# Attention plus gated FFN on one core: the last batch's third gate and up moved ahead of the products of the batch before it, batch 0's third gate and up given a bank pair that is free earlier, and the last scores put behind V products and zeros

## The reference, cut to what matters

```python
qkv = x @ w_qkv                                   # x (8, 512, 128), w_qkv (128, 384)
att = softmax(where(causal, q @ k.T / sqrt(8), -inf))
x = layernorm(x + att @ v)
gate = x @ (w_gate / 127).T; up = x @ (w_up / 127).T      # (8, 512, 384)
x = layernorm(x + (silu(gate) * up) @ (w_down / 127).T)
```

## Time and profile before

| | us |
|---|---|
| median of 3 executions | 364.29 |
| lowest, highest of them | 361.03, 364.29 |
| the profiled execution, its own time | 362.71 |
| span of its profile (first to last instruction) | 361.0 |
| attention, up to the last score matmul | 0 to 296.4 |
| from there to the first matmul of `gate_up(1, 0)` | 296.4 to 306.9 |
| FFN of the batches 1 to 7 up to the last matmul | 306.9 to 353.1 |
| last norm and store | 353.1 to 361.0 |

### The profile page before, as it was taken

One profiled execution on the slowest core, in us unless ns is written; L12 is line 12 of the kernel. 1 busy time (PEld: TensorE's weight loads), 2 busy tenths in 40 slices (PEclk: granted clock), 3 DMA queues, 4 the chain that ended last, 5 costly groups with the idle time before them and its releaser, 6 DMA issues.

```text
span 361.0 us, 9029 instructions
## 1 busy us (share of the span) xinstructions
PE 338.2 (94%) x2907; PEld 198.4 (55%) x2911; DVE 291.8 (81%) x1247; ACT 214.6 (59%) x277; POOL 180.2 (50%) x329
## 2 busy tenths in 40 slices
PE   4878999999999999999999999999999998999971
PEld 2533445556455645655564556556445544898961
DVE  6875658898888888988988898899898884868653
ACT  2400447877777677777867676876677774434310
POOL 8400133653384455447335734653433578787552
PEclk9996559999999999999999999999999969999997
DMA  4798330276337426532661553166200010011111
GB/s 145 279 301 246 83 86 5 63 254 190 91 126 229 120 63 236 155 112 86 228 190 37 188 170 120 33 237 202 66 4 5 5 30 3 1 36 53 46 44 58
DMA packets 33902, 41.73 MB, mean 116 GB/s; under 512 B 3136, under 2 KB 17472, under 8 KB 33856
## 3 DMA queue, kind: packets, MB, share of 16 engines
q1 hardware_dynamic: 33856, 41.17, 36.0%
HBM read 21.76 MB, written 18.87 MB: 113 GB/s over the span
## 4 chain that ended last, share of the span: by engine, by line
PE 79%; DVE 9%; issue 5%; DMA 3%; ACT 2%; POOL 1%; SPq 0%; DVEq 0%; POOLq 0%; ACTq 0%
PE psum L500 21%; PE psum L477 18%; PE psum L460 14%; PE psum L681 5%; DVE masked L853 5%; PE psum L416 5%; PE psum L407 4%; PE psum L669 3%; PE psum L671 3%; PE psum L442 2%; PE psum L509 2%; PE psum L432 2%; DMA scr_k<-parts 1%; DVE nm L853 1%; DMA xa<-L_attn_x 1%
## 5 line engine op out<-in xcount | busy, mean ns | idle before, releaser
L853 DVE CUSTOM_DVE_ANT_0 masked<-psum,mask 128x384 bf16<-128x384 f32 (+3 forms) x512 | 219.2, 487 | 37.5 <-PE psum L477 30.6
L756 ACT ACTIVATE pt<-psum 128x1024 f32<-128x1024 f32 x160 | 158.4, 1021 | 59.7 <-PE psum L460 59.2
L1028 POOL TENSOR_SCALAR_AFFINE_SELECT pt<-pt 128x512 f32<-128x512 f32 x128 | 79.7, 635 | 101.5 <-ACT pt L756 99.5
L477 PE MATMUL psum<-kx,qx 33*128 33x384 f32 (+3 forms) x512 | 93.5, 366 | 3.3 <-DMA kx<-scr_k 1.8
L500 PE MATMUL psum<-pt,vx 128*32 128x256 f32 (+2 forms) x1280 | 94.8, 397 | 0.1
L460 PE MATMUL psum<-qx,kx 35*128 35x384 f32 (+3 forms) x512 | 77.7, 353 | 0.9 <-DMA qx<-nm_T 0.8
L477 PEld LDWEIGHTS psum<-kx,qx 33*128 33x128 f32 x512 | 54.3, 193 | 40.9 <-DVE nm L853 19.1
L460 PEld LDWEIGHTS psum<-qx,kx 35*128 35x128 f32 x512 | 47.2, 192 | 30.4 <-issue 16.1
L500 PEld LDWEIGHTS psum<-pt,vx 128*32 128x32 f32 x1280 | 30.7, 110 | 39.0 <-issue 26.0
L853 DVE DVE_READ_ACCUMULATOR2_ANT nm<- 128x1 f32 x512 | 42.5, 83 | 0.0
L1016 POOL TENSOR_SCALAR nm_parts<-nm 128x16 fp32r<-128x16 f32 x32 | 6.6, 207 | 51.4 <-DVE nm L853 50.3
(11 more groups left out here) (64 smaller groups left out, 268.6 us busy)
## 6 DMA issues: line engine op xcount, KB each, us to landing
scr_q<-parts SPq DMA_DIRECT2D x16, 512.0 KB, 3.7
scr_k<-parts SPq DMA_DIRECT2D x16, 512.0 KB, 5.5
qx<-scr_q SPq DMA_DIRECT2D x64, 128.0 KB, 2.6
kx<-scr_k SPq DMA_DIRECT2D x64, 128.0 KB, 2.7
xa<-L_attn_x SPq DMA_DIRECT2D x8, 256.0 KB, 3.3
res<-L_attn_x SPq DMA_DIRECT2D x8, 256.0 KB, 2.8
out<-yo SPq DMA_DIRECT2D x8, 256.0 KB, 2.3
qx<-nm_T SPq DMA_DIRECT2D x64, 8.0 KB
```

Source lines behind the costliest of these rows:

```text
L477: last = pe.matmul(bank[:, col:col + width], qx[u][at:at + KM, 2 * g + hh // 2, P * i:P * i + P].bitcast(F32R), kx[u][at:at + KM, 2 * g + ...
L756: act.activation(pt[G % 2][:, 2 * s:2 * s + 2, :], pair_of("S", G, s), ACT.Exp, scale=SM_SCALE).then_inc(exp_done, 1)
L853: dve.tensor_tensor_reduce(masked[count % 4][:, 0:width], bank[:, col:col + width], mask[:, T - width:T], -1.0, 3.0e38, ALU.add, ALU.min, ...
L1028: pool.affine_select(out=blocks, in_=blocks, pattern=[[0, HG], [1, P]], compare_op=ALU.is_ge, fill=0.0, base=0, channel_multiplier=-1).the ...
```

## The change

**TensorE.** V products "0a" of group 30 go ahead of scores(31, 0), and three matmuls of zeros between them; "0b" ahead of scores(31, 1); two zeros ahead of scores(31, 2); "1" ahead of scores(31, 3). In the FFN, the bank pair of gate_up becomes a function of batch and m: batch 0 has pairs 0, 1, 0 for m = 0, 1, 2, the later batches 1, 2, 0, so that gate_up(0, 2) waits only for hidden(0, 0), and stands ahead of turn_out(15) instead of behind it; the wait for `attn_made` 16 and `ot_copied` 16 goes to gate_up(1, 1). For batch 7, gate_up(7, 2) goes ahead of down(6), and down(7) writes bank 6 instead of bank 4, with waits for the x1 of batch 7 instead of `r2_made`.

**VectorE.** hidden(7, 2) goes ahead of residual2(6); the norm of batch 6 is applied here (last_norm2(6)), behind residual2(7) and ahead of last_norm2(7).

**GpSimd.** For batch 6 only inverse2(6) is left.

```diff
--- before.py
+++ after.py
@@ -299,9 +299,17 @@
 
 
 
-        x1_ps, y_ps = psum[:, 6, :], psum[:, 4, :]
+        x1_ps = psum[:, 6, :]
+
+        def y_ps(c):
+            return psum[:, 4, :] if c < B - 1 else x1_ps
+
         last_pair = SCORE_TURNS.index(("S", GROUPS - 1, SLOTS - 2)) % 2
-        ff_ps = [(psum[:, 2 * p, :], psum[:, 2 * p + 1, :]) for p in (last_pair, 1 - last_pair)] + [(psum[:, 5, :], pv_ps)]
+        ff_pairs = [(psum[:, 2 * p, :], psum[:, 2 * p + 1, :]) for p in (last_pair, 1 - last_pair)] + [(psum[:, 5, :], pv_ps)]
+
+        def ff_ps(c, m):
+
+            return ff_pairs[(0, 1, 0)[m] if c == 0 else (1, 2, 0)[m]]
 
         block = ctx.enter_context(nc.Block())
 
@@ -656,42 +664,51 @@
                     transposes4(x1_ps, res[:, NB * c:NB * c + NB, :].rearrange("p n c -> p (n c)")).then_inc(x1_turned, 1)
 
             def gate_up(c, m):
-                if c > 0:
+                if c > 1:
                     pe.wait_ge(hid_made, HC * (c - 1) + m + 1)
-                elif m < 2:
-                    pe.wait_ge(exp_done, SLOTS * GROUPS - 1 + m)
-                else:
+                elif c == 1 and m == 1:
                     pe.wait_ge(attn_made, 2 * B)
                     pe.wait_ge(ot_copied, 2 * B)
+                elif c == 1:
+                    pe.wait_ge(hid_made, 2 + m // 2)
+                elif m == 2:
+                    pe.wait_ge(hid_made, 1)
+                else:
+                    pe.wait_ge(exp_done, SLOTS * GROUPS - 1 + m)
                 for n, full in enumerate((gate_full, up_full)):
                     w = wT[:, n, P * m:P * m + P].bitcast(F32R)
                     pe.wait_ge(x1_hi_made, c + 1)
-                    pe.matmul(ff_ps[m][n], w, x1_hi[c % 2][:].bitcast(F32R), start=True, stop=False)
+                    pe.matmul(ff_ps(c, m)[n], w, x1_hi[c % 2][:].bitcast(F32R), start=True, stop=False)
                     pe.wait_ge(x1_lo_made, c + 1)
-                    pe.matmul(ff_ps[m][n], w, x1_lo[c % 2][:].bitcast(F32R), start=False, stop=True).then_inc(full, 1)
+                    pe.matmul(ff_ps(c, m)[n], w, x1_lo[c % 2][:].bitcast(F32R), start=False, stop=True).then_inc(full, 1)
 
             def down(c):
                 pe.wait_ge(hid_made, HC * c + HC)
                 if c == 0:
                     pe.wait_ge(attn_made, 2 * B - 1)
+                elif c < B - 1:
+                    pe.wait_ge(r2_made, c)
                 else:
-                    pe.wait_ge(r2_made, c)
+                    pe.wait_ge(x1_hi_made, B)
+                    pe.wait_ge(x1_lo_made, B)
                 for m in range(HC):
                     for n in range(NB):
-                        last = pe.matmul(y_ps[:, C * n:C * n + C], hid[c % 2][:, m, P * n:P * n + P],
+                        last = pe.matmul(y_ps(c)[:, C * n:C * n + C], hid[c % 2][:, m, P * n:P * n + P],
                                          wT[:, 2, P * m:P * m + P], start=(m == 0 and n == 0),
                                          stop=(m == HC - 1 and n == NB - 1), skip_group_check=True)
                 last.then_inc(y_full, 1)
 
 
             G = GROUPS - 1
+            values(G - 1, "0a")
+            add_zeros(3)
             scores(G, 0)
-            values(G - 1, "0a")
+            values(G - 1, "0b")
             scores(G, 1)
-            values(G - 1, "0b")
+            add_zeros(2)
             scores(G, 2)
+            values(G - 1, "1")
             scores(G, 3)
-            values(G - 1, "1")
             turn_x1(0)
             scores(G, 4)
             turn_out(2 * B - 2)
@@ -702,14 +719,17 @@
             gate_up(0, 1)
             values(G, "2")
             turn_x1(1)
+            gate_up(0, 2)
             turn_out(2 * B - 1)
-            gate_up(0, 2)
             for c in range(1, B):
                 gate_up(c, 0)
                 gate_up(c, 1)
+                if c == B - 1:
+                    gate_up(c, 2)
                 turn_x1(c + 1)
                 down(c - 1)
-                gate_up(c, 2)
+                if c < B - 1:
+                    gate_up(c, 2)
             down(B - 1)
 
         @block.scalar
@@ -814,7 +834,7 @@
                 act.wait_ge(gate_full, k + 1)
                 if k > 1:
                     act.wait_ge(hid_made, k - 1)
-                act.activation(sg[k % 2][:], ff_ps[m][0], ACT.Silu, scale=W_SCALE).then_inc(silu_done, 1)
+                act.activation(sg[k % 2][:], ff_ps(c, m)[0], ACT.Silu, scale=W_SCALE).then_inc(silu_done, 1)
 
             for s in range(SLOTS - 1):
                 exp_slot(GROUPS - 1, s)
@@ -940,14 +960,14 @@
                         dve.wait_ge(pv_piece, PIECES * (GROUPS - 1 + c))
                     else:
                         dve.wait_ge(y_full, c - 1)
-                dve.tensor_tensor(hid[c % 2][:, m, :], ff_ps[m][1], sg[k % 2][:], ALU.mult).then_inc(hid_made, 1)
+                dve.tensor_tensor(hid[c % 2][:, m, :], ff_ps(c, m)[1], sg[k % 2][:], ALU.mult).then_inc(hid_made, 1)
 
             def residual2(c):
                 u = c % 2
                 dve.wait_ge(y_full, c + 1)
                 if c > 1:
                     dve.wait_ge(yo_made, NB * (c - 1))
-                dve.scalar_tensor_tensor(r2[u][:].rearrange("p n c -> p (n c)"), y_ps, W_SCALE * W_SCALE,
+                dve.scalar_tensor_tensor(r2[u][:].rearrange("p n c -> p (n c)"), y_ps(c), W_SCALE * W_SCALE,
                                          res[:, NB * c:NB * c + NB, :].rearrange("p n c -> p (n c)"),
                                          ALU.mult, ALU.add).then_inc(r2_made, 1)
                 dve.wait_ge(r2_made, c + 1)
@@ -980,10 +1000,14 @@
                 hidden(c, 1)
                 if c == 1:
                     stats1(B - 1)
+                if c == B - 1:
+                    hidden(c, 2)
                 low_x1(c + 1)
                 residual2(c - 1)
-                hidden(c, 2)
+                if c < B - 1:
+                    hidden(c, 2)
             residual2(B - 1)
+            last_norm2(B - 2)
             last_norm2(B - 1)
 
         @block.gpsimd
@@ -1121,10 +1145,11 @@
             norm1(3, 2)
             inverse1(4, B - 1, B)
             norm1(4, 3)
-            for c in range(B - 1):
+            for c in range(B - 2):
                 norm2(c)
                 if c + 5 < B:
                     norm1(c + 5, 3 if c + 5 < B - 1 else 4)
+            inverse2(B - 2)
             inverse2(B - 1)
```

## The result

The changed kernel takes 358.34 us in the median of 6 executions, the kernel before 364.29 us beside it; the ratio is 0.985 with a 95% interval of 0.980 to 0.990. Ratios here leave out the executions that took over 1.5% longer than the fastest of their kernel, medians don't. A second set of six, beside the experiments, gave 361.09 us and a ratio of 0.988 (0.982 to 0.994). All twelve together have a median of 360.12 us. The forecast was 360.4 with a range of 358.3 to 362.9, so 358.34 lies just above the lower edge of the range.

The account below looks back on a forecast made before the run. It took TensorE to bound the kernel (busy 94% of the span), except at the end. 362.71 - 2.1 (end) - 0.54 (transition) = 360.07 us; half of 0.79 us for scatter between executions made 360.4, range 358.3 to 362.9.

Parts of the forecast that it names:

- The end: Last batches: gate_up(7, 2) ahead of down(6) removes TensorE's 1.86 us idle time ahead of down(7); -2.1 us.
- the second bank: At down(7): with bank 6 it needn't wait for residual2(6), which would cost about 0.9 us.
- the norm in the hole: Batch 6's norm, 1.11 us on VectorE, fits its 1.81 us idle time while GpSimd works; cost 0.
- the page of the Trainium skill that the prediction weighed: VectorE's two-port mode and GpSimd take turns at a common port; up to 1.0 us lost beside the power.
- The transition: From attention to FFN: V products and zeros ahead of the last scores, gate_up(0, 2) earlier, clock full; -0.54 us.
- VectorE as the next bound: Transition: x1_lo(0) stays at 299.5, so TensorE waits 1.4 us for it and most of the full clock's gain is lost.
- The clock falls as before: Rival at the transition: granted clock drops again, +1.5 us there, 362.1 us in all; chance 0.25.
- The rival of the slower side: FFN: two new 1.4 us waits for VectorE make the clock fall, losing 3.3 us; 363.4 us; chance 0.08.
- Sum of the transition, -0.54: Total from attention to the FFN's first matmuls, -0.54 us, with bounds of -0.6 and +1.7 us.
- Sum of the end, -2.1, bounds -2.3 and -1.4: Total for the last batches, down(6) to the final store: -2.1 us, between -2.3 and -1.4.
- the forecast's own range: Whole kernel: 358.4 to 361.8 us, from lowest and highest known times, 361.03 and 364.29, each less 2.64; chance 0.58.

Follow-up runs that it names:

- e4: Changed kernel with the norm of batch 6 applied by GpSimd again; ratio 0.986 to the kernel before.
- e7: Changed kernel with the statistics of batches 5 and 6 moved on VectorE behind low_x1(0); ratio 0.979 to the kernel before.
- e6: Changed kernel with turn_out(15) ahead of gate_up(0, 2) again; ratio 0.986 to the kernel before.
- after: The changed kernel itself, in its first set of six executions; 358.34 us, ratio 0.985 to the kernel before.
- c1: The changed kernel run again, unchanged, beside the experiments; 361.09 us, ratio 0.988 to the kernel before.
- e8: Changed kernel with both moves, statistics later (e7) and turn_out(15) first (e6); 358.20 us, ratio 0.978 to the kernel before.
- e2: Changed kernel with the end part taken back, so the transition part alone; 363.45 us, ratio 0.991 to the kernel before.
- e10: e8 run again, unchanged; 356.74 us, ratio 0.979 to the kernel before.
- e1: Changed kernel with the transition part taken back, so the end part alone; 360.72 us, ratio 0.994 to the kernel before.
- e3: Changed kernel without its five matmuls of zeros; 362.44 to 378.97 us in four executions, no ratio.
- e9: e8 without the five zeros; no ratio; from the wait's end to the x1_lo(1) matmul 18.11 us against 15.04.

## Why the prediction was right

**The end** (-2.1 forecast, -2.05 measured). Each step came as worked out: gate_up(7, 2) 0.38 us after the last matmul of gate_up(7, 1), behind hidden(6, 2); four products on VectorE in one row, ready ahead of residual2(6); TensorE without a gap; 0.9 us for the second bank (0.88 of wait, 1.1 in all); the norm in the hole for nothing. By the page of the Trainium skill that the prediction weighed (SBUF — State Buffer, "SBUF: two separate sides") up to 1.0 us would have been lost there, by the rows 0.2 at most; the trace shows 0.04. So it doesn't bear out that one of the two stood still for a whole instruction of the other: VectorE's four took 1.11 us as alone, though the power began in their midst. Whether they use the two-port mode of which the page speaks, no view shows. With 0.79 us left in the hole it would have needed more than that to matter, and e4 shows that the other place for the norm costs 0.84.

**The transition** (-0.54 forecast, -0.51 measured against the same execution). The reasoning with VectorE as the next bound held: x1_lo(0) didn't come earlier in relation to the wait, and most of the clock's gain went into a wait of 1.16 us (forecast 1.4). e7 shows this by moving the bound and nothing else. That putting gate_up(0, 2) ahead of turn_out(15) has a price was seen too: 0.53 us by e6.

**The rivals.** "The clock falls as before" didn't come true in the changed kernel's profiles. Of the nine profiles with the changed order and its zeros, seven (after, c1, e4 to e8) have no low clock in this stretch, e2 and e10 have 3.4 us of it each. The rival of the slower side needed the new idle times of 1.2 to 1.3 us to cost clock in the FFN; at both the clock stayed at 1.00:

```profile
295.90:297.05 1.15, 0.00 (x1) 0.00 (x1) 1.02 (x2) 0.19 (x1) 1.15 (x3) 1.00 0.05 14
302.90:304.18 1.28, 0.00 (x1) 0.01 (x1) 1.25 (x4) 0.00 (x0) 0.50 (x1) 1.00 0.00 0
```

**What was mis-sized.** The term "Sum of the transition, -0.54" was worked out against one execution, in which the clock was low for 6.8 us there. I had its variation only in the early stretch. e1 shows an execution of the old order with a longer one, which costs 1.3 us more (18.83 against 17.49). "Sum of the end, -2.1, bounds -2.3 and -1.4" has the same gap: I never asked what the old wait of 1.86 us does to the clock of the matmuls behind it, and e2 shows 1.38 us, outside my bounds. So the two parts are worth 2.6 us against the profiled execution and up to 1.85 + 3.43 = 5.3 us against one that loses both, which no profile shows. This, and the early stretch, in which the first six executions happened to do well (the second six had a median of 361.09), are what can lie between the forecast of 360.4 and 358.34; they weren't forecast, and without the luck of the first six the measured time is 360.12 (all twelve). How the 2.1 us divide between them isn't settled by these runs: only profiles, one for each kernel, tell the stretches apart. Two smaller slips are in the sums: 364.29 - 2.64 is 361.65, not the 361.8 at which the forecast's own range ends, and the bound of -2.3 for the end stands on no row.

## What to carry to other kernels

Where two executions of the same instructions differ by several us, split the traces at an instruction ahead of the first change: here nearly half of the difference between the profiles lay before anything had changed. The price of a lost clock is what TensorE loses less what it would have waited anyway. At the same length of low clock, 3.4 us, it was 0.10 us with VectorE as the next bound (e2, 17.08 against 16.98) and 1.51 us once that bound was moved (e10, 16.55 against 15.04). Leaving out the zeros cost 0.47 us in the one case and 3.07 in the other, but there the low stretch was also longer, 10.2 us against 6.8. So such fillers are to be judged again after the neighbours are cleared. And work that moves off a path often uncovers the next queue in order; a look at which of its entries aren't needed yet (two batches' statistics here) gave 1.4 us for no instruction more.

## What the runs showed of the hardware

Matmuls of zeros can help to hold the granted clock at full, though they compute nothing: with five of them behind a wait of 0.8 us it stayed at 1.00 in seven profiles of nine, without them it fell in both profiles of the new order (e3, e9) and in all three of the old. But zeros among score-like work didn't raise it early on: 23.9 us at 0.50 with TensorE busy for 23.57 of them.

A low clock can last long in the midst of dense work. In e3's profile it lay at half for some 34 us of the attention stage, in code that the change doesn't touch:

```profile
262.50:297.00 34.50, 34.15 (x207) 15.71 (x208) 19.34 (x90) 15.10 (x18) 8.76 (x18) 0.51 0.03 10
```

That execution took 378.97 us. One execution of e8 had a mean clock of 0.541 and took 510.77 us, where four of the other five took 355 to 359. What set this off no run here shows.
